# Four graph layers in a software pipeline: the attention half starts half a turn later and is cut into finer steps

## The reference

```python
h = relu(LN(x))                                   # L0: hypergraph convolution, twice
H = (adj != 0); Dn = 1 / (H @ adj[0]); Be = 1 / H.sum(0)
z = LN(relu(Dn * (H @ (Be * (H.T @ (h @ W1.T)))) + b1))
x = x + Dn * (H @ (Be * (H.T @ (z @ W2.T)))) + b2 + h
h = relu(LN(x))                                   # L1: two hops over a softmax-like transition
T = rownorm(adj * exp(leaky_relu(sj + si + ab)))
x = x + relu(h @ Wk0 + (T @ h) @ Wk1 + (T @ T @ h) @ Wk2 + bk)
h = relu(LN(x)); Xp = h @ Wp                      # L2: 8 heads of 32
x = x + relu(tanh(adj * (Xp C Xp.T)) @ Xp)
h = relu(LN(x))                                   # L3
x = x + relu((adj @ h) @ K3) * mask
```

## Time and profile before

| | us |
|---|---|
| median of 3 runs (lowest, highest) | 1734.43 (1731.84, 1736.19) |
| the profiled execution | 1734.22 |
| its span, first to last instruction | 1732.1 |
| PE busy | 1490.9 (86%) |
| DVE busy | 1162.4 (67%) |
| ACT busy | 897.6 (52%) |
| POOL busy | 233.9 (14%) |

### The profile page before, as it was taken

The page is one execution under the profiler, slowest core; times in us unless marked ns, Lnnn a source line. Parts: engine busy times, 40 slices in busy tenths (PEclk is TensorE's granted clock), DMA queues, the critical chain, the costliest instruction groups (busy, mean ns, idle before and its releaser), DMA issues.

```text
span 1732.1 us, 26278 instructions
## 1 busy us (share of the span) xinstructions
PE 1490.9 (86%) x9850; PEld 1091.1 (63%) x9850; DVE 1162.4 (67%) x2512; ACT 897.6 (52%) x1479; POOL 233.9 (14%) x151
## 2 busy tenths in 40 slices
PE   3678898988989898898989889898988989898864
PEld 3576574866757486675748667574866747576632
DVE  5556668667676866767676676777677677766632
ACT  2235656464564645556464555646455564645442
POOL 2002020201103020120302002030210203021000
PEclk8889999999999999999999999998999999999987
DMA  6010110201111020111102011110201111020010
GB/s 187 1 49 19 50 55 19 83 5 49 55 49 55 9 82 11 48 54 48 54 1 89 12 48 54 48 54 0 91 12 48 54 48 54 0 73 12 0 37 12
DMA packets 50084, 75.15 MB, mean 43 GB/s; under 512 B 4032, under 2 KB 23040, under 8 KB 50048
## 3 DMA queue, kind: packets, MB, share of 16 engines
q1 hardware_dynamic: 50048, 74.66, 12.7%
HBM read 66.27 MB, written 8.39 MB: 43 GB/s over the span
## 4 chain that ended last, share of the span: by engine, by line
PE 75%; DVE 11%; ACT 8%; issue 5%; POOL 0%; DMA 0%; POOLq 0%; ACTq 0%; DVEq 0%
PE ring_f L992 45%; PE ring_b L992 13%; PE ring_b L1251 6%; PE pv_acc L1267 5%; DVE att L942 4%; ACT att L588 2%; PE ring_f L1165 1%; PE ring_f L1075 1%; PE ring_f L1134 1%; ACT xp_t L571 1%; DVE rows L881 1%; ACT hf L542 1%; PE ring_b L1239 1%; PE ring_b L1276 1%; DVE rows L901 1%
## 5 line engine op out<-in xcount | busy, mean ns | idle before, releaser
L942 DVE TENSOR_TENSOR att<-ring_b,at 128x1024 f32<-128x1024 f32 x256 | 300.7, 1216 | 48.8 <-PE ring_b L1251 48.2
L588 ACT ACTIVATE att<-att 128x1024 f32<-128x1024 f32 x256 | 261.9, 1072 | 112.8 <-DVE att L942 109.1
L415 POOL TENSOR_TENSOR rstd<-var,mhalf 128x4 f32<-128x4 f32 x80 | 80.7, 1009 | 1285.4 <-DVE var L729 1285.4
L1267 PE MATMUL pv_acc<-att,xp_n 128*32 128x512 f32 x1024 | 151.3, 666 | 61.4 <-ACT att L588 61.4
L1251 PE MATMUL ring_b<-xc_t,xp_t 32*128 32x512 f32 x1024 | 159.4, 694 | 47.7 <-DVE att L942 46.6
L992 PE MATMUL ring_f<-w,uz 128*128 128x256 f32 (+1 forms) x896 | 187.0, 332 | 4.7 <-DVE w L645 4.6
L992 PE MATMUL ring_f<-m,tr_h 128*128 128x256 f32 x1024 | 187.8, 285 | 0.0
L743 DVE TENSOR_TENSOR m<-ring_f,m 128x512 fp32r<-128x512 f32 (+1 forms) x128 | 70.6, 551 | 170.4 <-ACT m L452 170.0
L992 PEld LDWEIGHTS ring_f<-m,tr_h 128*128 128x128 f32 x1024 | 159.5, 192 | 12.6 <-issue 12.6
L992 PEld LDWEIGHTS ring_f<-w,uz 128*128 128x128 f32 x896 | 151.7, 191 | 19.8 <-DVE w L645 4.7
L457 ACT ACTIVATE m<-ring_f,be 128x256 fp32r<-128x256 f32 x128 | 53.7, 470 | 188.6 <-PE ring_f L992 186.8
(11 more groups left out here) (148 smaller groups left out, 2646.0 us busy)
## 6 DMA issues: line engine op xcount, KB each, us to landing
rows<-in_adjT SPq DMA_DIRECT2D x16, 1024.0 KB, 5.4
adj_n<-in_adj SPq DMA_DIRECT2D x16, 1024.0 KB, 5.3
at<-in_adjT SPq DMA_DIRECT2D x16, 1024.0 KB, 5.3
x_in<-in_x SPq DMA_DIRECT2D x16, 512.0 KB, 6.1
out_x<-xb SPq DMA_DIRECT2D x16, 512.0 KB, 2.9
wrow<-in_adj SPq DMA_DIRECT2D x16, 256.0 KB, 6.1
att<-in_Wk SPq DMA_DIRECT2D x3, 256.0 KB, 7.1
att<-in_W2T SPq DMA_DIRECT2D x1, 512.0 KB, 4.5
```

Of the source, the lines that this page charges most:

```text
L415: pool.tensor_tensor(rstd[k][:], var[k][:], mhalf[:], ALU.pow).then_inc(rstd_made[k].sem, 1)
L588: act.activation(v, v, ACT.Tanh).then_inc(tanh_made.sem, 1)
L942: dve.tensor_tensor(att[:, u % 2, 2 * half:2 * half + 2], ring_b[half][:], at[:, u % NT].unsqueeze(1).broadcast_to([P, 2, N]), ALU.mult)\
L1267: ins = pe.matmul(pv_acc[h * KH:(h + 1) * KH, :], xp_n[:, t, ch:ch + KH], att[:, u % 2, h], start=(t == 0), stop=(t == NT - 1), skip_group ...
```

## The change

The k half is moved by half a turn. On PE its head (now beside `f_y`, `f_hT` and `f_sj`) and the scores of units 0 to 3 with the attends of 0 and 1 (now between the hop steps) keep delay 1. The rest of units 2 to 7 and the tail have delay 2: the units run beside `f_m`, `f_u`, `f_conv1`, `f_zT` and `f_xw`, `k_outT` beside `f_m2`, `k_ax` and `k_out` in the logits stage. Before, turn 16 holds all units of graph 15 and turn 17 the end of its tail; now turn 16 holds the end of graph 14's units, its tail, and the head and first units of graph 15, and turn 17 the rest. `all_turns` has one more turn on either side of the loop.

For this, `at2`, a second copy of adjT in SBUF, feeds `k_ax`; `at` is free after the last unit. `hb` and `h3` become two tiles, `y_part` shares `h3`, and `ax_s` shares `xc_s`. A new ACT step `k_keep` copies `xa` to `xb`, so that the next graph's `f_x2` may write `xa`. Many steps are cut finer: the normalisations, `k_xp`, `k_xc`, `k_xn`, `k_outT`, `k_ax`, `k_out`, `f_m`, `f_u`, `f_conv1`, `f_zT`, `f_xw`, `f_m2`, `f_y`, `f_hT`, `f_tt` by tile or part, POOL's `f_h0`, `f_sum`, `k_y` into four pieces each.

```diff
-        ax_s = sb("ax_s", [P, 4, N], F32R)
+        ax_s = xc_s[:].rearrange("p a (c n) -> p (a c) n", c=2)
-        y_part = att[:, 1, 0:2].rearrange("p t (u d) -> p (t u) d", d=D)
+        y_part = h3
-            for b in (0, 1, 2, 3):
+            for b in (0, 1, 2, 3, 4):
-            with engine.Fori(4, G) as b:
+            with engine.Fori(5, G) as b:
-            for b in (G, G + 1, G + 2):
+            for b in (G, G + 1, G + 2, G + 3):
...
+            def next_at2(g):
+                if seen(g, 1):
+                    if seen(g, 1):
+                        sp.wait_ge(ax_full.sem, ax_full.after(g, 2, ago=1))
+                    load_at2(g)
...
             def turn(b):
                 run_turn(b, G, (
-                    (1, next_adjt), (2, next_at), (0, next_x), (0, next_wrow), (3, store), (0, next_adj),
+                    (1, next_adjt), (2, next_at), (0, next_wrow), (3, next_at2), (4, store), (0, next_x),
+                    (0, next_adj),
                 ))
...
+            def k_keep(g):
+                act.wait_ge(x2_out.sem, x2_out.after(g, 2))
                 if seen(g, 1):
+                    act.wait_ge(y_made.sem, y_made.after(g, NT, ago=1))
+                copy(xb[:], xa[:], kept)
...
+            def k_y(g, i):
+                pool.wait_ge(o_made.sem, o_made.after(g, i // 2 + 1))
+                pool.tensor_tensor(y_part[:, i], y_part[:, i], xb[:, i], ALU.add).then_inc(y_made.sem, 1)
...
             def k_scores(g, u):
                 part, t = divmod(u, NT)
                 if u == 0:
                     pe.wait_ge(xc_made.sem, xc_made.after(g, 1))
                     pe.wait_ge(xn_made.sem, xn_made.after(g, 1))
+                    if seen(g, 1):
+                        pe.wait_ge(ax_lo.sem, ax_lo.after(g, 2, ago=1))
+                    if seen(g, 1):
+                        pe.wait_ge(o_made.sem, o_made.after(g, 2, ago=1))
...
+            def k_ax(g, c, half):
+                if c == 0 and half == 0:
+                    pe.wait_ge(at2_loaded.sem, at2_loaded.after(g, 1))
+                    pe.wait_ge(h_made[H3].sem, h_made[H3].after(g, NT))
                     pe.wait_ge(gated.sem, gated.after(g, 2 * UNITS - 1))
...
+                ins = products(ring_b[0][:, c], [(h3[:, t, c * P:(c + 1) * P], at2[:, t])
+                                                 for t in (2 * half, 2 * half + 1)], half == 0, half == 1)
+                if half == 1:
                     ins.then_inc(ax_full.sem, 1)
```

The tables of PE, ACT, DVE and POOL are rewritten; one line of PE's new one:

```diff
+                    (0, f_conv1, 3), (2, k_attend, 4), (2, k_scores, 6), (2, k_attend, 5), (2, k_scores, 7),
```

More of the change, by code:

```diff
@@ new lines, in f_u, with f_conv1 @@
+            def f_u(g, c):
+                v = slice(c * N, (c + 1) * N)
+                dve.wait_ge(u_hi.sem, u_hi.after(g, c + 1))
+                low(uz[:, 1, v], bank_of(U, c)[:], uz[:, 0, v], u_lo)
+            def f_conv1(g, i):
+                if i == 0:
+                    if not seen(g, 1):
+                        set_up()
+                    dve.wait_ge(c_dn.sem, c_dn.after(g, c_dn.per))
+                dve.wait_ge(conv_full.sem, conv_full.after(g, i + 1))
+                dve.scalar_tensor_tensor(rows[:, i], bank_of(CV, i)[:], dn[:, i:i + 1], b1_bc[:], ALU.mult,
+                                         ALU.add).then_inc(conv_out.sem, 1)
@@ L837, in f_zT @@
+            def f_zT(g, k):
+                v = slice(k * N, (k + 1) * N)
+                dve.wait_ge(z_hi.sem, z_hi.after(g, k + 1))
+                low(m2[:].rearrange("p a n -> p (a n)")[:, v], bank_of(ZT, k)[:],
+                    uz[:].rearrange("p a n -> p (a n)")[:, v], z_lo)
+                if k == HT_ - 1 and not seen(g, 1):
                     set_up_weights()
@@ new lines, in f_u @@
+            def f_u(g, k):
+                pe.wait_ge(inct_made.sem, inct_made.after(g, 2 * k + 2))
+                pe.wait_ge(m_lo.sem, m_lo.after(g, k + 1))
+                for c in range(2):
+                    ps = bank(g, U, c) if k == 0 else bank_of(U, c)
+                    ins = products(ps[:], [(m2[:, part, j * D + c * P:j * D + (c + 1) * P], inc_t[:, j])
+                                           for j in (2 * k, 2 * k + 1) for part in (0, 1)], k == 0, k == 1)
+                    if k == 1:
+                        ins.then_inc(u_full.sem, 1)
@@ L1087, in xw, with f_xw @@
                 return ins
[L1089 to L1090 removed]
+            def f_xw(g, s):
+                if s == 0:
                     bank(g, XW, 0)
@@ new lines, in f_y @@
+            def f_y(g, half):
+                pe.wait_ge(m2_lo.sem, m2_lo.after(g, half + 1))
+                for k in range(2):
+                    ps = bank(g, Y, k) if half == 0 else bank_of(Y, k)
+                    for i in (2 * k, 2 * k + 1):
+                        ins = products(ps[:, (i % 2) * D:(i % 2 + 1) * D],
+                                       [(inc_t[:, j, i * P:(i + 1) * P], m2[:, part, j * D:(j + 1) * D])
+                                        for j in (2 * half, 2 * half + 1) for part in (0, 1)],
+                                       half == 0 and i % 2 == 0, half == 1)
+                    if half == 1:
+                        ins.then_inc(y_full.sem, 1)
```

814 lines of the change are left out of this document (388 added, 426 removed).

## The result

The changed kernel takes 1711.2 us (median of 4 runs, 1708.1 to 1713.9) against 1734.3 (4 runs, 1731.8 to 1736.2): a ratio of 0.987, 95% interval 0.984 to 0.989. That is 23 us or 1.3% faster, and beyond the 0.3% that can be told from no change. "No real change" was wrong.

What follows compares the result with a forecast made beforehand. PE was taken as the bound, busy for 86% of the span, its waits being what a new order can win. From 1734.2 us: steady turns -5, fill -6, drain +12, giving 1735, own range 1722 to 1748, rivals included 1706 to 1766.

Steps and rivals of the forecast that it cites:

- No real change: Main forecast for the whole kernel: no real change in the turn, 1735 us, range 1722 to 1748; chance 0.36.
- the walk's sum: Steady turn traced step by step: 9.5 us of PE waits, 99.5 us per turn before adding the clock fall.
- PE's own steps: PE's steps in a steady turn, kept as long as before: 90.2 us in the step-by-step trace.
- the floor of 89.4: Products in a turn: 101.5 us less 10.4 of PE waits and 1.7 for the clock fall.
- The clock term: One PE clock fall per turn, at 46 to 57 us beside Z's layer norm, adding 1.7 us: turn 101.2.
- The fill: Turns 0 and 1: about 1 us saved by finer f_hT and 5 us in turn 1; -6 us.
- The drain: After the last hop: graph 15's first scores 16 to 18 us later, finer tail -4; +12 us.
- the clock stays up: Rival for the steady turns: no clock fall, turn 99.5 us, kernel 1712 us; chance 0.30.
- two falls: Rival: two clock falls per turn, at 46 to 57 and 78 to 100 us; turn 102.9, kernel 1759; chance 0.23.
- x comes too late: Rival: x load queued behind other transfers lands at 75 us, delaying DVE; 28 us slower, 1763; chance 0.11.
- no wait of PE at the hops: First 46 us of a steady turn, f_tt and hop steps to f_conv1: PE waits for nothing.
- The second adjacency copy: The at2 load adds 16 MB; its cost was taken to be only its place in the transfer queue.

Runs made afterwards that it cites:

- clock_after: Changed kernel plus nine small products of constants on PE in the waits beside Z's layer norm; 1697.3 us, ratio 0.978.
- dve_at_logits: Changed kernel plus one unused 128x512 DVE step behind the last maximum of the logits stage; 1714.8 us.
- clock_before: Kernel before the change plus eight small products of constants on PE ahead of scores 3; 1727.9 us, ratio 0.996.
- dve_at_sums: clock_after plus one unused DVE step between the row sums and the low part of k_ax 1; 1713.2 us.
- x_first: clock_after with the load of x issued ahead of at, wrow, at2 and the store; 1692.6 us, ratio 0.977.
- dve_at_hops: Changed kernel plus one unused 128x512 DVE step beside the hops, ahead of unit 3's gate; 1714.5 us.
- one_at: x_first without the second adjacency copy at2: k_ax reads at, whose next load is issued behind it; 1693.1 us.
- coarse_steps: clock_after with PE's order and waits at the logits put back together, the half-turn move kept; 1723.6 us, ratio 0.995.

## Why the prediction was wrong, step by step

- **The failed step is the walk's sum.** I had 99.5 us of turn without the clock; `clock_after`, which has no fall, shows 98.07. The waits that I named are there and in their places, but they are shorter: 1.4 ahead of `k_out` instead of 2.5, 0.8 for `f_hT` instead of 1.4, 0.8 for `k_xn` instead of 0.95, and 2.9 at Z's layer norm (attends 1.3, scores 1.4, 0.2 at a low part) instead of 4.2; the 0.5 at `f_q` is as foretold. Together 6.4 against 9.5. The mechanism was right and the sizes were not. One fault may be seen in the rows of `dve_at_logits` above: a step of 0.68 us on a DVE that is fed without a gap is followed by the next after 0.60. The walk took such an overlap off for the gates and, by its text, for nothing else. Whether this is what makes the waits too long, over a chain such as mask, sums, low part, is argued and not shown. 14 x 1.43 is 20 us.
- **PE's own steps hid a part of that error.** The walk gave them 90.2 us, took the floor of 89.4 as the truth, and subtracted 0.25. The two turns without a fall have 91.0 and 91.1 us of PE, so the walk had 0.8 too little and not 0.8 too much. "The change leaves PE's work as it is" holds for the number of products and not for the time: 1512.7 us against 1490.9. In part this is only how the record shows a group that is cut: the transposes of `f_hT`, 1.09 us in one piece before, are there as three pieces of 0.73, 0.33 and 0.77. Where the rest comes from is open.
- **The clock term was mis-sized.** The fall is there, once in most turns and where I put it, but it costs 1.0, not 1.7. The 1.7 was read off the slow products of before, and as busy time it is about right: where turns with and without a fall can be compared, it adds 1.3 to 1.6 us to PE's busy time. What it costs is another matter. In the kernel before it was 0.5, because without the fall PE comes to `f_hT` too early, and waits there for what it won. The row is not among those of the turn of the earlier trace rows, which has a fall at the units; it is in `clock_before` and, word for word, in the turn of before that starts at 318.18:

```profile
PE ring_f L1134 <- ACT hf L462: 0.9, 1, 0.9
```

  14 x 0.7 is 10 us.
- **The fill** was -6 and is -1.8. I set the forecast of turn 1, 93.5, against a window of 98.7 that runs past the end of the hops into the next `k_ax`; from hop end to hop end the turn before takes 93.9. The forecast of the turn itself (93.5 against 92.8) was good. An error of 4 us.
- **The drain** was +12 and is +16.9. Scores 0 of graph 15 start 45.0 us behind the last hop, not at 42 to 44 (rows below). The delay arises ahead of `k_ax`, which starts at 32.4 instead of 29: `k_xp` starts 1.9 later than in the walk and takes 4.58 us instead of 3, with the granted clock at 0.50 for 3.4 us of it. Eight units then take 33.2 against 32.3, with three sets of scores at half clock (2.09 us) instead of two, and the tail got 3.3 shorter, for which I had 4. POOL's last sum runs 2.80 us in four pieces instead of 2.34, but starts on halves. An error of 5 us, 1 of it because 16 to 18 less 4 is 12 to 14, and I took the low end.

```profile
1604.28 1.06 PE L1288 MATMUL pv_acc<-att,xp_n 128*32 128x512 f32 x8
...
1627.16 4.58 PE L1013 MATMUL ring_b<-xc_s,wp 128*128 128x512 f32 x12 [2.02 <-DVE xc_s L784]
...
1636.63 7.10 PE L1013 MATMUL ring_b<-at,h 128*128 128x512 f32 x16 [1.30 <-ACT h L482]
1645.14 3.07 PE L1013 MATMUL ring_b<-k,xc_s 128*128 128x256 f32 x24 [1.41 <-DVE xc_s L784]
1649.29 1.14 PE L1272 MATMUL ring_b<-xc_t,xp_t 32*128 32x512 f32 x8 [1.08 <-ACT h L639]
```

With the sizes mended: 1735 - 20 - 10 + 4 + 5 = 1714, the profiled 1713.9. These sizes are the measured ones, so the sum must close and proves nothing. The turn was forecast 30 us too slow, the fill and the drain 9 too fast; without these 9 the forecast would have been 1744.

- **Rival "the clock stays up".** It gave nearly the right time, 1712, by luck: the clock did fall, and without a fall the turn is 98.07 and not its 99.5. Had it stayed up, the kernel would have taken 1697.
- **Rival "two falls", 1759.** Of the twelve turns between the marks one has two falls, one at 31 and one at 61 us from its mark, and takes 100.7 us instead of 99.1; two have none (97.8 and 98.2). The section of the Trainium skill that I weighed ("TensorE: Matmul & The Clock Gate", section "A second HAM failure mode: psum-queue depth-cycling") says, of another kernel, that short idles between groups of products make the clock fall again and again. The trace agrees as to one fall in most turns, and `dve_at_sums` shows how little is missing for the second place. The two falls together cost 2.7 (100.7 against 98.0), not 3.4: the second alone 1.6, which is near the rival's 1.7, the first 1.1. "In the old turn the fall comes after the longest wait" holds for eight turns of twelve; in the other four it comes at 78 us, at the end of the logits stage.
- **Rival "x comes too late".** Half right. x landed 9.6 us after its own issue, which is 12.3 us after that of `at` (844.07 to 856.38): the 12 that I took from the rate of two loads. DVE waited 0.75 for it in the row above, 0.5 to 1.0 over the turns, where I had x half a microsecond behind DVE. The later landing, which made the price of 28 us, did not come. The wait cost about 0.35 us a turn. That the last gate releases x too was wrong: its tile is free at least 13.5 us earlier (`x_first`).
- **Right**: no wait of PE at the hops (`dve_at_hops` shows DVE's slack there). The second adjacency copy costs nothing once x is issued ahead of it (`one_at` against `x_first`); no run tests it in the changed kernel's own order, where it stands ahead of x, and none tests `k_keep`. POOL's pieces cost it 3.9 us a turn (18.5 instead of 14.6), where I had 3.

## What to carry to other kernels

A walk finds the places of the waits; here it overstated them by half (9.5 against 6.4) and understated PE's steps. Closing the same walk over the known kernel first might show such an excess; no run here tells. Look at the turns one by one before you price a clock fall: the turns of before that differ in its place had the answer. What counts is what stands behind it: where the next wait shrinks by the time lost, it is nearly free; where it does not, it cost up to 1.8 here, and a few products of constants in the waits ahead of it can be worth 0.8% of the kernel. When a pipeline gets deeper, look at the drain by itself: its order is inherited from the loop, where banks are shared and work lies beside it, and neither holds there. And look whether an issue in SP's table stands behind waits that it does not need.

## What the runs showed of the hardware that was not expected

- The same 3.4 us at half clock adds 1.3 to 1.6 us to PE's busy time (91.0 to some 92.4 in the changed kernel, 90.8 to 92.3 in `clock_before`, 92.5 to 94.1 in `coarse_steps`), but costs the turn 1.6 to 1.8 at 62 us behind the mark (a turn of the changed kernel, one of `coarse_steps`), 1.4 at 76 us (`dve_at_sums`), 1.0 at 31 us, and in the kernel before 0.5 at 59 us and 0.1 at 78. At a margin it comes in some turns only: behind `k_out`'s wait of 1.4 us none of `clock_after`'s twelve turns has it, behind one of 2.0 us (`dve_at_sums`) three of twelve.
- Nine products of 128x256 (1.8 us of PE) spread over three waits of a stretch removed the fall in every turn. They cost nothing that shows: the two turns of the changed kernel without a fall take 97.8 and 98.2 us, those of `clock_after` 97.8 to 98.2.
- Five transfers issued within 2.7 us land in the order of issue: in the changed kernel `at` after 5.2 us, `wrow` 6.5, `at2` 8.4, the store 9.1 and x 9.7 (the turn with its issues at 844.07 to 846.72). `at`, the first, takes what 1 MB takes alone (5.3). x alone took 3.5.
- A 0.68 us step on DVE, put in at four places of one turn, cost 0, 0, 0.46 and about 0.5 us: the engine's share of busy time, 72%, says nothing of which.
